# First attention of a two-attention block: products for row maxima from 64 rows each, issued in pairs

## The reference

```python
q = jnp.einsum('bsd,hqd->bhsq', x, w_q)
k = jnp.einsum('bsd,hqd->bhsq', x, w_k)
v = jnp.einsum('bsd,hvd->bhsv', x, w_v)
scores = jnp.einsum('bhsq,bhtq->bhst', q, k)
masked = jnp.where(causal, -jnp.inf, scores)
weights = jax.nn.softmax(masked / jnp.sqrt(jnp.float32(dq)), axis=-1)
out = jnp.einsum('bhst,bhtv->bhsv', weights, v)
cat = out.transpose(0, 2, 1, 3).reshape(b, s, -1)
return jnp.einsum('bsf,df->bsd', cat, w_o)
```

## Time and profile before

| | |
|---|---|
| median of 3 runs | 2683.82 us (2676.89 to 2683.84) |
| the profiled execution | 2687.63 us, span 2685.6 us |
| first attention in the span | about 57 to 1330 us |
| granted TensorE clock over the span, mean | 0.944 |
| TensorE, VectorE, ScalarE, GpSimd busy over the span | 2347.9, 1705.8, 1461.6, 1026.2 us |

### The profile page before, as it was taken

One profiled execution on the slowest core, in us unless ns is written; L12 is line 12 of the kernel. 1 busy time (PEld: TensorE's weight loads), 2 busy tenths in 40 slices (PEclk: granted clock), 3 DMA queues, 4 the chain that ended last, 5 costly groups with the idle time before them and its releaser, 6 DMA issues. The chain is left out here.

```text
span 2685.6 us, 45555 instructions
## 1 busy us (share of the span) xinstructions
PE 2347.9 (87%) x12882; PEld 1429.0 (53%) x12882; DVE 1705.8 (64%) x4489; ACT 1461.6 (54%) x3224; POOL 1026.2 (38%) x1795
## 2 busy tenths in 40 slices
PE   4999999999999999999836589999999757999990
PEld 2555566555665556655533233333333555888880
DVE  5776663777546674576358777777777375444445
ACT  3566663666546664566437477777777543333332
POOL 0344442554334443454505322222222104555554
PEclk8999999999999999999878699999999877999995
DMA  3011110111101110011123311111011442111115
GB/s 106 17 29 25 29 40 12 27 29 45 25 19 25 29 35 25 19 29 29 23 75 132 134 35 35 35 35 31 24 33 35 149 122 77 52 52 52 52 48 192
DMA packets 141572, 135.56 MB, mean 50 GB/s; under 512 B 74400, under 2 KB 111008, under 8 KB 139680
## 3 DMA queue, kind: packets, MB, share of 16 engines
q1 hardware_dynamic: 132128, 113.84, 14.2%
q0 software_dynamic: 9216, 18.96, 2.4%
HBM read 87.58 MB, written 33.88 MB: 45 GB/s over the span
## 5 line engine op out<-in xcount | busy, mean ns | idle before, releaser
L288 POOL TENSOR_TENSOR a_A<-a_A,a_P 128x512 f32<-128x512 f32 (+3 forms) x320 | 317.3, 991 | 289.0 <-PE a_O L594 278.2
L1234 ACT ACTIVATE b_P<-b_SC 128x512 f32<-128x512 f32 (+3 forms) x768 | 328.7, 497 | 162.8 <-PE b_SC L1337 161.3
L442 ACT ACTIVATE a_P<-a_SC 128x512 f32<-128x512 f32 (+3 forms) x640 | 292.1, 469 | 202.1 <-PE a_SC L577 195.4
L500 DVE CUSTOM_DVE_ANT_0 a_MX<-a_MX,a_causal 128x128 f32<-128x128 f32 (+3 forms) x512 | 248.5, 501 | 154.8 <-PE a_MX L646 149.3
L576 PE MATMUL a_SC<-a_QR,a_KR 128*128 128x512 f32 (+3 forms) x768 | 318.1, 418 | 4.3 <-DMA a_QS<-a_minusT 2.9
L1176 POOL TENSOR_SCALAR_AFFINE_SELECT b_P<-b_P 128x128 f32<-128x128 f32 x512 | 146.6, 293 | 442.8 <-ACT b_P L1234 433.2
L1284 DVE CUSTOM_DVE_ANT_0 b_MX<-b_MX,b_causal 128x128 f32<-128x128 f32 (+3 forms) x512 | 248.4, 498 | 79.8 <-PE b_MX L1386 77.5
L646 PE MATMUL a_MX<-a_KR,a_QR 128*128 128x512 f32 (+3 forms) x768 | 282.8, 377 | 17.5 <-DVE a_peak L500 14.3
L1386 PE MATMUL b_MX<-b_K,b_Q 96*128 96x512 bf16 (+3 forms) x768 | 251.3, 339 | 42.5 <-ACT b_Q L1245 14.5
L327 POOL TENSOR_SCALAR_AFFINE_SELECT a_P<-a_P 128x128 f32<-128x128 f32 x448 | 144.5, 329 | 345.4 <-ACT a_P L442 342.0
L577 PE MATMUL a_SC<-a_QS,a_KS 65*128 65x512 f32 (+3 forms) x768 | 265.5, 350 | 0.0
(11 more groups left out here) (265 smaller groups left out, 4407.3 us busy)
## 6 DMA issues: line engine op xcount, KB each, us to landing
a_inv<-inv_rows SPq DMA_DIRECT2D x128, 128.0 KB, 3.0
stack_rows<-p_stk SPq DMA_DIRECT2D x32, 480.0 KB, 2.7
a_W<-in_w_pair SPq DMA_DIRECT2D x34, 384.0 KB, 3.8
b_stk<-stack_rows SPq DMA_DIRECT2D x136, 96.0 KB, 2.2
W<-in_w SPq DMA_DIRECT2D x8, 1024.0 KB, 7.5
c_E<-done_rows SPq DMA_DIRECT2D x8, 1024.0 KB, 6.6
n_x<-in_x SPq DMA_DIRECT2D x4, 1024.0 KB, 9.2
a_xT<-hold SPq DMA_DIRECT2D x4, 1024.0 KB, 5.0
```

Source lines behind the costliest of these rows:

```text
L288: eng.tensor_tensor(acc[h][c][:, a:], acc[h][c][:, a:], buffer(n, h)[:, a:], ALU.add).then_inc(added[h], 1)
L442: act.activation(buffer(n, h)[:, a:], SC[h][:, a:], ACT.Exp, scale=DH1 ** -0.5).then_inc(s["exp_done"], 1)
L500: dve.tensor_tensor_reduce(MX[c % MAX_BANKS1][:, 0:w], MX[c % MAX_BANKS1][:, 0:w], causal[:, BANK - w:], 1.0, 3 * NEG, ALU.add, ALU.max, p ...
L1234: act.activation(probs[k % RING2][:, a:], SC[k % SCORE_BANKS][:, a:], ACT.Exp, scale=DH2 ** -0.5).then_inc(s["exp_done"], 1)
```

## The change

`MAXN` now puts the two heads' products of the same queries and keys next to each other. `maxima_of_both` issues both: head h's takes only its own 64 rows of `QR` and `KR`, so rounded q by rounded k, without the remainder; head 0's lie in the rows 0 to 63, head 1's in 64 to 127. One wait ahead of them asks for the reduction of product c-2, which gives the second of the two banks free. `MAX_COUNT` has even numbers now, and a slot's pairs come behind the scores: in a slot with four products one pair behind each head's scores, else one pair behind the scores of head 1. None is left behind a projection. VectorE takes its list from the same tables.

```diff
-MAXN = [(h, i, c) for first, c0 in ((True, 0), (False, 0), (False, 1)) for h in range(2) for i, c in MAXU
-        if (i < BANK // P) == first and c == c0]
+MAXN = [(h, i, c) for first, c0 in ((True, 0), (False, 0), (False, 1)) for i, c in MAXU
+        if (i < BANK // P) == first and c == c0 for h in range(2)]
 NMAX = len(MAXN)
 MAX_BANKS1 = 3
-MAX_COUNT = (3, 3, 2, 3, 3, 2, 2, 2, 2, 2, 0, 0)
+MAX_COUNT = (4, 2, 2, 4, 2, 2, 2, 2, 2, 2, 0, 0)
...
-            def maximum(n1, p, c):
-                h, i, ch = MAXN[c]
+            def maxima_of_both(n1, p, c):
+
+                i, ch = MAXN[c][1:]
...
-                pe.wait_ge(s["max_used"], n1 * NMAX + c + 1)
-                if c == NMAX % MAX_BANKS1:
+                if c == 0:
 
                     pe.wait_ge(s["turn_copied"], n1 + 1)
-                bank = MX[c % MAX_BANKS1]
-                pe.matmul(bank[:, 0:w], QR[p][h][:, i * P:(i + 1) * P], KR[p][h][:, ch * BANK:ch * BANK + w],
-                          start=True, stop=True).then_inc(s["max_ready"], 1)
+                pe.wait_ge(s["max_used"], n1 * NMAX + c + 2)
+                for h in range(2):
+                    own = slice(DH1 * h, DH1 * (h + 1))
+                    pe.matmul(MX[(c + h) % MAX_BANKS1][:, 0:w], QR[p][h][own, i * P:(i + 1) * P],
+                              KR[p][h][own, ch * BANK:ch * BANK + w], start=True, stop=True).then_inc(s["max_ready"], 1)
...
-                    def one_max():
-                        if maxima:
-                            maximum(n1, p, maxima.pop(0))
+                    def one_pair():
+                        maxima_of_both(n1, p, maxima[0])
+                        del maxima[:2]
...
                             scores(n2, 1 - p, n, h)
-                        one_max()
+                        if len(maxima) > 2 * (1 - h):
+                            one_pair()
...
-                    one_max()
...
-                    while maxima:
-                        one_max()
```

## The result

| | before | after |
|---|---|---|
| median | 2681.98 us (4 runs, 2676.89 to 2683.84) | 2804.95 us (4 runs, 2803.23 to 2811.27) |
| the profiled execution | 2687.63, span 2685.6 | 2811.27, span 2809.2 |
| granted TensorE clock, mean | 0.944 | 0.931 |
| first attention, first to last turn of the maxima | 81.6 to 1298.5 us | 90.7 to 1424.4 us |

After by before is 1.0464, with a 95% interval of 1.0445 to 1.0483. The change makes the kernel 123 us slower. Forecast were 80 slower, 2764, with a range up to 2805: the sign is right, the median stands at the very edge of the range, and a third of the loss isn't in my sum.

A forecast was written before the change was run, and what follows sets the result against it. TensorE was taken to bound the step (busy 35.89 of 36.33 us). Waits of 2.43 plus 0.15 us make 2.58 a step, times 31 is 80 us, added to the 2683.8 median: 2764 us, range 2695 to 2805.

The forecast's parts named there:

- The price that no row shows: Entering and leaving half-row shape on TensorE: bounded by 0.02 and 0.22 us, taken as 0.22, with pairs fully overlapping.
- The rival of free changes: Changing to half rows costs 0.02 us, not 0.22; waits stay: 0.47 us a step, 2699 us; chance 0.14.
- the one of no overlap: Rival: a pair's halves don't overlap, each takes its full columns: 1.92 us more a step, 2824 us; chance 0.10.
- Slot 1: The slot's pair waits for reduction 2 on VectorE, so the k projection behind it starts 2.24 us late.
- Slots 2 and 3: Delayed scores, ScalarE copies and VectorE's split hold reduction 8 and a pair; the v projection starts 2.43 us late.
- slots 4 to 9: Remaining pairs, reductions in time: shape changes bring 2.66 us of products to 2.81, so 0.15 us more.
- The sum per step: Steady step of the first attention: 2.43 us late plus 0.15 gives 2.58 us more, over 31 steps 80 us.
- One sign: In the profile after, loads of the 384-column pairs and slot 3's second pair wait for VectorE, each over 0.7 us.
- The granted clock is 1.00, so the 2.4 GHz level throughout: Read from one steady step of the kernel before, 36.33 us long, in saying what bounds it.
- In the first step VectorE bounds the products: taken as 0, within 2: First step of the first attention: no added time counted, within 2 us, as VectorE bounds it.
- The rival of the faster side: Free changes and no loss by waits: 68 us less, 2616 us, if added waits stay under 2.20 a step; chance 0.08.

The follow-up runs named there:

- two reduce-first runs: VectorE's slot-0 reductions put ahead of its splits of q: in the changed kernel 2716.99 us (1.0125), in the kernel before 2668.62 us (0.9942).
- The filler: Changed kernel plus two thrown-away full-row products (512 and 384 columns) ahead of slot 1's waiting pair: 2766.09 us, 1.032 of the kernel before.
- The longer wait with full rows: Changed kernel's order with all 128 rows, slot 1's pair also waiting for one reduction it doesn't need: 2776.35 us, 1.0356 of the kernel before.
- best half-row version: Changed kernel with the second pair of slots 0 and 3 and slot 1's pair moved to the slot's end: 2702.5 us, 1.0081 of the kernel before.
- short filler: Changed kernel plus one thrown-away product of 256 columns ahead of slot 1's waiting pair: 2767.93 us, 1.0329 of the kernel before.
- full rows: Changed kernel's order, pairs and waits, but both products over all 128 rows: 2744.62 us, 1.0237 of the kernel before.

## Why the prediction was right and where it failed

- *The price that no row shows.* Right: 0.22, and full overlap. A pair of 512 columns in a steady step, on TensorE:

```profile
624.87 0.40 PE L577 MATMUL a_SC<-a_QS,a_KS 65*128 65x512 f32 x1
625.20 0.49 PE L648 MATMUL a_MX<-a_KR,a_QR 64*128 64x512 f32 x2
625.62 1.98 PE L620 MATMUL a_PK<-hold,a_W 128*128 128x512 f32 x4
```

  From the correction product of 512 columns to the pair it is 0.33, not 0.23: a stop of 0.10. From the pair to the next record it is 0.42, and those are 0.11 for the load that isn't ahead, 0.21 for 512 columns and 0.10 to 0.11 for the stop on the way out. The second product of a pair starts 3 to 4 ns behind the first. The rule of the Trainium skill, "TensorEngine Tiling (Array Packing)", Key Properties, that a change of the mode drains TensorE, holds for two tiles of rows as it did for the cut by columns. That a load for another row group is pulled ahead (the Trainium skill, "TensorE: Matmul & The Clock Gate", Part 3) doesn't show across such a change: each pair's load lies open with its 0.11. The text on record was too quick to rest a rival on that rule: the product ahead of a pair takes 65 or 128 rows, so rows of both halves, and the pair's load is not for another row group than those in use. The rival of free changes fell with the 0.10 and 0.11, the one of no overlap with the 3 to 4 ns.
- *Slot 1.* Right: 2.24 late against a measured 2.27, by the chain from ScalarE's copies through the split to reduction 2. VectorE in a step with a fall:

```profile
611.86 0.69 DVE L513 TENSOR_TENSOR a_QS<-a_PV,a_QR 64x512 fp32r<-64x512 f32 x1 [0.92 <-ACT a_QR L399]
612.58 0.43 DVE L500 CUSTOM_DVE_ANT_0 a_MX<-a_MX,a_causal 128x256 f32<-128x256 f32 x1
```

  The pair's load at 613.12 comes 0.54 behind the start of this reduction; 0.52 was the row's number. The two reduce-first runs show that the order on VectorE makes this chain.
- *Slots 2 and 3, slots 4 to 9.* Right: 13.59 and 0.16 against 13.57 and 0.15. The sum per step, 2.58, came out at 2.57. One sign was missed: the second pair of slot 3 was to wait over 0.7, and waits 0.48 (its load queue 0.62).
- *"The granted clock is 1.00, so the 2.4 GHz level throughout".* The step that failed. It was true of the step of before that I read, and I priced after's waits as idle time alone. The wait of slot 1 leaves TensorE idle for 1.5 us (its load queue for 1.8), and behind it the clock falls from 2.4 to 1.2 GHz in 23 windows of 31. Missing from the sum: 21 falls more than before by 1.67 us, 35 us. The filler shows it: in the middle steps the falls are gone and everything else is in place. Of its 39 us some 5 are the first step's, and the other 34 are close to the 35 of the falls. The longer wait with full rows shows it from the other side.
- *"In the first step VectorE bounds the products: taken as 0, within 2".* Mis-sized: 9.1 us. VectorE did bound it in before (16.96 of 18.28 us), and the text took that to hold in after. There the pairs and their reductions wait for each other with nothing between them (5.6 us more of waits on TensorE), and the clock is low. With the filler, which stands only in slot 1, it was 4.2.
- *The rival of the faster side.* It asked for added waits under 2.20 us a step. Even where three pairs stand behind the slot's other work the half rows cost 0.67 a step against full ones, and the best half-row version stayed at 2702.5 us, so no order of the waits among those I tried with half rows would have saved it.

In all: of the 123 us some 55 (31 steps by 1.78) are the new order's waits, 24 the changes of shape net of the saved columns, 35 the falls of the clock, and 9 the first step.

## What to carry to other kernels

Products of 64 rows side by side, alone between full-height work, don't pay: a pair of 512 columns takes 0.63 us with both changes (0.10 + 0.42 + 0.11), two full-height ones in sequence take 0.46. By these prices two pairs in a row would take 0.84 to 0.95, depending on whether the second pair's load lies open, against 0.92 for four full-height products: an estimate, which no run here tried. A wait that is added on the engine that bounds must be priced twice, as idle time and by what TensorE's clock does behind it, and the record behind the wait is where to look (2.97 for 1.98 us). Where banks are few, put the reductions that free them ahead of work that waits for a third engine: here a change of order on VectorE alone gave 1.2%.

## What the runs showed of the hardware that I had not expected

The granted clock fell from 2.4 to 1.2 GHz behind a single idle time of some 1.5 us in a step. The number of windows of 31 with a clock under 1.00, by the idle time of TensorE ahead of pair 4/5 in a row of that run:

| run | rows | idle ahead of the pair, us | windows with a fall |
|---|---|---|---|
| after | 64 | 1.47 to 1.49 | 23 |
| filled wait | 64 | none | 1 |
| short filler | 64 | 1.05 | 3 |
| full rows | 128 | 1.34 | 4 |
| full rows, longer wait | 128 | 1.74 | 17 |

A fall costs 1.67 us in a middle step of after and 1.63 in one with the longer wait. Steps with the same rows and the same waits fall in one case and not in the next (38.90, 40.60, 40.56, 38.94 above), so it can't be told from one step. Each count is of one execution, some of the windows cover a change of batch or the first or last step, and the runs' clean steps differ in length (38.1 to 38.9 us). After and its two fillers have clean steps of the same length, and there 23 falls against 1 and 3 are the wait's doing; the counts with full rows, 4 and 17, are less sure, and their order against 23 isn't shown. A load of weights with 64 rows takes 183 ns in the median, one with 128 rows 190: half the rows don't halve it.
